# Deformable convolutions: the clamp of the distances on POOL instead of DVE, and the middle one of three sampled parts read by DVE instead of ACT

## The reference

```
_block: h      = relu(conv3x3(x))
        offset = conv3x3(h)                       # 9 taps x (y, x) per pixel
        x      = relu(deform_conv(h, offset, w))  # bilinear samples of h, then a sum over taps and channels
layers 1 to 3 take x + (input of the layer before)
final:  cat(x, input) (64 channels) -> offset = conv3x3 -> deform_conv, added to the input
```

## Time and profile before

| | |
|---|---|
| median of 3 runs | 4874.02 us (4866.67 to 4875.91) |
| profiled execution, its own time | 4847.23 us |
| its span | 4845.4 us |
| mean granted TensorE clock | 0.913 |
| chunks of the layer steps | 8 x 32, starts of the sums some 8.5 us apart |
| chunks of the final steps | 2 x 32, some 26 us apart |

### The profile page before, as it was taken

How to read it: one execution, slowest core, us unless ns; L and a number is a source line. 1 busy time by engine, 2 the same in 40 slices (tenths; PEclk the granted TensorE clock), 3 DMA queues, 4 the chain that set the end, 5 groups by cost and what they waited for, 6 DMA issues and landing times.

```text
span 4845.4 us, 204328 instructions
## 1 busy us (share of the span) xinstructions
PE 4248.1 (88%) x73184; PEld 3301.6 (68%) x73184; DVE 2918.2 (60%) x5838; ACT 2784.3 (57%) x6651; POOL 1143.4 (24%) x655
## 2 busy tenths in 40 slices
PE   4997997898798798798799799698989887999988
PEld 3775675676576576576576577577777776777777
DVE  4884784785685686686586587354444535554544
ACT  2893884785685586586587488244343433344433
POOL 0441341341341242242243143011111101111110
PEclk8998998899899899899899799799899998888998
DMA  3442442442442442443343343744444436444442
GB/s 123 121 125 74 121 125 76 117 125 69 125 125 72 121 124 78 119 125 86 110 125 92 102 125 103 185 111 109 101 109 109 100 92 157 112 103 107 111 111 77
DMA packets 253669, 533.42 MB, mean 110 GB/s; under 512 B 61488, under 2 KB 161328, under 8 KB 235824
## 3 DMA queue, kind: packets, MB, share of 16 engines
q1 hardware_dynamic: 253072, 524.86, 41.1%
HBM read 468.16 MB, written 56.45 MB: 108 GB/s over the span
## 4 chain that ended last, share of the span: by engine, by line
PE 79%; issue 8%; SPq 6%; ACT 2%; DMA 2%; DVE 2%; POOL 1%; POOLq 0%; ACTq 0%; PEld 0%; DVEq 0%; PEldq 0%
PE P L531 30%; PE PS L545 25%; PE PS L557 17%; PE P L502 6%; SPq L383 2%; SPq L375 2%; ACT H L790 1%; DMA HB<-off_store 1%; PE PS L502 1%; DMA off_store<-FOFF 1%; ACT YC L727 1%; DVE FOFF L974 1%; DVE ST L977 0%; DVE ST L978 0%; PE P L517 0%
## 5 line engine op out<-in xcount | busy, mean ns | idle before, releaser
L857 DVE TENSOR_TENSOR A<-P,YC 121x384 f32<-121x384 f32 (+1 forms) x4608 | 2313.5, 551 | 1327.0 <-ACT YC L727 1041.9
L531 PE MATMUL P<-HL,SEL 32*121 32x384 f16 (+1 forms) x21504 | 1738.6, 309 | 336.3 <-issue 236.3
L727 ACT ACTIVATE YC<-P 121x384 f32<-121x384 f32 (+1 forms) x4608 | 1739.8, 439 | 100.4 <-PE P L531 88.5
L531 PEld LDWEIGHTS P<-HL,SEL 32*121 32x121 f16 (+1 forms) x21504 | 1195.1, 119 | 734.1 <-issue 420.5
L545 PE MATMUL PS<-A,VT 121*32 121x144 f32 (+1 forms) x32768 | 1339.3, 304 | 71.5 <-issue 47.4
L545 PEld LDWEIGHTS PS<-A,VT 121*32 121x32 f32 (+1 forms) x32768 | 963.4, 115 | 381.9 <-issue 202.0
L1038 POOL CAST HL<-DIST 128x1152 f16<-128x1152 f32 x320 | 365.8, 1143 | 3437.3 <-DVE DIST L862 3203.8
L704 ACT ACTIVATE SMP<-PS 128x432 f32<-128x432 f32 (+1 forms) x1152 | 567.5, 493 | 722.7 <-PE PS L545 721.8
L557 PE MATMUL PS<-SMP,CW 128*128 128x128 f32 x6912 | 856.6, 280 | 5.2 <-ACT SMP L704 5.2
L557 PEld LDWEIGHTS PS<-SMP,CW 128*128 128x128 f32 x6912 | 795.7, 192 | 87.3 <-issue 76.9
L1040 POOL TENSOR_TENSOR HL<-DIST,HL 128x1152 f16<-128x1152 f32 x320 | 769.3, 2404 | 135.2 <-issue 76.0
(11 more groups left out here) (56 smaller groups left out, 581.2 us busy)
## 6 DMA issues: line engine op xcount, KB each, us to landing
HB<-off_store SPq DMA_DIRECT2D x2560, 72.0 KB, 2.4
VT<-ht_store SPq DMA_DIRECT2D x256, 512.0 KB
VT<-ht_store SPq DMA_DIRECT2D x768, 132.0 KB
VT<-ht_store SPq DMA_DIRECT2D x256, 88.0 KB
ht_store<-A SPq DMA_DIRECT2D x80, 256.0 KB, 3.4
off_store<-FOFF SPq DMA_DIRECT2D x160, 128.0 KB, 2.5
A<-x_dram SPq DMA_DIRECT2D x2, 2048.0 KB, 10.2
H<-x_dram SPq DMA_DIRECT2D x2, 2048.0 KB, 15.6
```

The lines of the kernel that those rows point to most:

```text
L531: mm = nc.tensor.matmul(dst, SEL[q, table, 0:sh.npos], hats, start=part == 0, stop=part == 1)
L727: nc.scalar.activation(YC[0:sh.npos, g % X_SLOTS, 0:sh.size], P[0:sh.npos, g % Y_SLOTS, 0:sh.size], ACT.Copy).then_inc(y_ready, 1)
L857: return nc.vector.tensor_tensor(dst, x, y, ALU.mult)
```

## The change

The clamp leaves DVE's queue (behind product 1, and ahead of offset item 4) and stands on POOL ahead of the cast: POOL waits for the abs, clamps, waits for its own clamp, casts, and subtracts as before. In kind 0 with one source (the layer steps), the part with index 1 is no longer read by ACT behind its copy of g = 7 but by DVE behind product 7, by a `tensor_copy` from PSUM. The final steps keep all reads on ACT; their clamp moves too. In the tail of a step, DVE's read stands between the two last residuals.

```diff
--- before.py
+++ after.py
@@ -88,6 +88,8 @@
         self.after = {2: [4, 9], 3: [4, 7, 10], 6: [2, 4, 6, 8, 10, 11]}[count]
 
         self.sum_after = 1
+
+        self.dve_parts = [1] if count == 3 and kind == 0 else []
 
         self.lag = 3 - self.batches
         self.ps_uses = self.batches * count + 1
@@ -732,7 +734,7 @@
                                 continue
                             else:
                                 prev = (c - 1, sh.batches - 1)
-                            if g in sh.after:
+                            if g in sh.after and sh.after.index(g) not in sh.dve_parts:
                                 read_part(*prev, sh.after.index(g))
                             if b == sh.batches - 1 and g == sh.sum_after and before >= sh.lag:
                                 read_sum(c - sh.lag, (half + sh.lag) % 2)
@@ -741,7 +743,8 @@
                     if sh.lag == 2:
                         read_sum(CHUNKS - 2, 0)
                     for k in range(nparts):
-                        read_part(CHUNKS - 1, sh.batches - 1, k)
+                        if k not in sh.dve_parts:
+                            read_part(CHUNKS - 1, sh.batches - 1, k)
                     read_sum(CHUNKS - 1, 1)
 
                 chunk_loop(act, body, tail)
@@ -856,11 +859,6 @@
                     y = y.broadcast_to(list(x.shape))
                 return nc.vector.tensor_tensor(dst, x, y, ALU.mult)
 
-            def clamp(c):
-
-                dve.wait_ge(abs_done, c + 1)
-                nc.vector.tensor_scalar(DIST[:, :], DIST[:, :], SCALE, SCALE, ALU.min, ALU.subtract).then_inc(clamp_done, 1)
-
             def body_of(sh, layer, group, final):
                 nparts = len(sh.parts)
 
@@ -870,6 +868,12 @@
                     x = P[0:sh.npos, Y_SLOTS + g % X_SLOTS, 0:sh.tiles * sh.size].rearrange("p (n a) -> p n a", n=sh.tiles)
                     a = A[0:sh.npos, half if sh.kind == 0 else b, :].rearrange("p (n a) -> p n a", n=sh.tiles)
                     return product(sh, a[:, :, at:at + sh.size], x, YC[0:sh.npos, g % X_SLOTS:g % X_SLOTS + 1, 0:sh.size])
+
+                def read_part(c, k):
+                    w, s = sh.parts[k][0]
+                    count = len(sh.parts[k])
+                    dve.wait_ge(ps_full, c * sh.ps_uses + k + 3)
+                    nc.vector.tensor_copy(smp_px(0, sh, w, s, count), PS[:, 0:TAPS * BPX * count]).then_inc(ps_free, 1)
 
                 def add_residual(c, band, half):
 
@@ -889,8 +893,8 @@
                             dve.wait_ge(y_ready, n + 1 + Y_SLOTS)
                             dve.wait_ge(x_full, n + 2)
                             one_product(g, b, half).then_inc(product_done, 1)
-                            if b == 0 and g == 1 and not last:
-                                clamp(c + 1)
+                            if before > 0 and b == 0 and g in sh.after and sh.after.index(g) in sh.dve_parts:
+                                read_part(c - 1, sh.after.index(g))
                             if before >= sh.lag and b == sh.batches - 1 and g == sh.sum_after + 2:
                                 if sh.lag == 2:
                                     add_residual(c - 2, band - 1, half)
@@ -900,6 +904,8 @@
                 def tail():
                     if sh.lag == 2:
                         add_residual(CHUNKS - 2, BANDS - 1, 0)
+                    for k in sh.dve_parts:
+                        read_part(CHUNKS - 1, k)
                     add_residual(CHUNKS - 1, BANDS - 1, 1)
 
                 def input_back(c, band, half, before, last):
@@ -965,8 +971,6 @@
                 for n in range(ITEMS):
 
                     unit, image = divmod(n, IMG)
-                    if n == IMG:
-                        clamp(0)
                     dve.wait_ge(off_full, unit + 1)
                     if n >= OFF_SLOTS:
 
@@ -1034,6 +1038,8 @@
 
             def hats(c, half):
 
+                wait_alone(pool, abs_done, c + 1)
+                nc.gpsimd.tensor_scalar(DIST[:, :], DIST[:, :], SCALE, SCALE, ALU.min, ALU.subtract).then_inc(clamp_done, 1)
                 wait_alone(pool, clamp_done, c + 1)
                 nc.gpsimd.tensor_copy(HL[:, 0, half, :], DIST[:, :]).then_inc(hat_step, 1)
                 wait_alone(pool, hat_step, c + 1)
```

## The result

The changed kernel takes 5446.75 us (median of 4 runs, 5431.56 to 5461.90) against 4870.35 (4864.88 to 4875.91): ratio 1.1183 [1.1149, 1.1218]. Slower was the likeliest side of the forecast, but 4902 is far off and the time lies 297 us above the top of the range. The profiled execution took 5445.4 us (span 5443.6; 4847.2 and 4845.4 before), so 598 us have to be found.

A forecast was written before the change was run, and what follows sets the result against it. The prediction took a resynchronised chunk of 8.5 us as the pitch, to be set by the third sample waiting for DVE's read. 29 + 1 - 2 = +28 us on 4874 gave 4902; forecast's own range 4885 to 4940, whole range 4860 to 5150.

The forecast's parts named there:

- The clock as no issue: Steady loop of the kernel before: granted clock 1.00, the 2.4 GHz level, so no clock loss was priced.
- Clamp off DVE: DVE's queue: removing the 0.75 us clamp saves 0 per chunk, and 2 us in all at step starts.
- Clamp onto POOL: POOL, ahead of the cast: POOL has time, order matters; with a 1.25 us clamp the residual just gets in.
- D: Duration of POOL's clamp: taken as 1.25 us, between ends of 0.75 and 2.41.
- A + 5.33 + D: Time the hats are ready on POOL, A being the start of the chunk's abs.
- Rival 1: POOL's subtraction gets ahead of DVE's residual: 5148 us with every second chunk hit, 5331 with every chunk; chance 0.22.
- knife edge: Residual against POOL's subtraction: at 1.25 us of clamp the subtraction starts 4.31 or 4.45 after the sums' start, residual 4.31.
- S + 4.31: Predicted start of DVE's residual in a chunk, S being the start of the sum matmuls.
- Rival 2: POOL's clamp is long, so the residual waits for the cast: 5009 us at 2.0 us, 5104 at 2.41; chance 0.13.
- Middle read onto DVE: DVE behind product 7: a 0.60 us read delays the third sample; 0.125 per chunk, 29 us over 232 chunks.
- Rival 3: DVE reads early enough for the third sample (start by S + 6.1), spreads lose their waits: 4823 us; chance 0.13.

The follow-up runs named there:

- late_only: Kernel before, with the layer steps' residual moved in DVE's queue behind the chunk's last product: 4868.95 us, ratio 0.9998.
- quick_late: Kernel before with a 1.15 us POOL multiply-and-add replacing DVE's clamp (values not clamped), reads on ACT, residual behind the last product: 4864.50 us, ratio 1.0002.
- quick2: Kernel before with two POOL multiplications (2.5 us together) replacing DVE's clamp, values not clamped; reads on ACT, residual in its old place: 5006.56 us, ratio 1.0327.
- after_late: Changed kernel with the layer steps' residual moved behind product 11, the chunk's last: 5405.95 us, ratio 1.1110.
- quick_both: Changed kernel with a 1.15 us multiply-and-add in place of POOL's clamp (values not clamped), middle read on DVE: 5472.60 us, ratio 1.1247.
- quick_clamp: Kernel before with a 1.15 us POOL multiply-and-add replacing DVE's clamp (values not clamped), all reads on ACT, residual in its old place: 5303.87 us, ratio 1.0894.
- clamp_only: Changed kernel with the middle read back on ACT, so only the clamp moves to POOL: 5284.60 us, ratio 1.0867.
- read_only: Kernel before with only the middle part's read moved to DVE, clamp still on DVE: 4981.51 us, ratio 1.0245.
- read_late: Kernel before with the middle read on DVE and the layer steps' residual behind product 11, clamp still on DVE: 4904.51 us, ratio 1.0077.

## Why the prediction was wrong

**The clock as no issue.** It was read from the kernel before and held for it. The forecast and every rival priced a late step by its own microseconds at the full clock. After the change PE stops in every steady chunk (0.66 us in the mean), and the sums' group is busy 1036.1 us instead of 856.6: 180 of the 598 us, 1.94 in a chunk whose sums are slow throughout and less in the others. The chunks that have such sums are longer by more than that, 12.2 instead of 9.71, together 264 us; what else than the clock makes them long is not separated. No rival had this term.

**Clamp off DVE: nothing gained.** This held. late_only against quick_late, 0.9998 and 1.0002, differ in little but where the clamp's time lies, although quick_late has no clamp on DVE at all.

**Clamp onto POOL: this step failed.** The term D, for which the forecast had ends of 0.75 and 2.41 and said "I take 1.25", measured 4.09. The form was not in the trace, and the bound from above was taken from another kind of instruction. The formula behind it was right: A + 5.33 + D gives A + 9.42, measured A + 9.44, and its condition, hats in time "for D up to 2.4", agrees with what was run: at D = 2.5 the granted clock stayed 1.00 and 8 sums of 256 were slow (quick2), at 4.09 PE waited for the hats. With the right D the step would have read: abs to abs 9.70, 232 x (9.70 - 8.5) = 278 us, and to that the half clock, which only a run gives.

**Rival 1.** In the changed kernel it is a small part of the cause (after_late gives back some 40 us). Its mechanism exists as described: at D = 1.15 residuals of 2.55 us end 0.15 behind the subtraction, and quick_late takes all of the price away. The forecast was wrong on where the knife edge lies; by its own numbers, residual and subtraction both at S + 4.31, it was a tie in one chunk of two. It counted on one chunk of two; 216 of 256 were hit: the chunk shown has sums at the full clock and both instructions start at S + 4.25, and behind sums at the half clock the residual comes later still, while the subtraction runs. Its price for the whole change with every chunk hit was 5331 (with D = 0.75 its formula gives delays of 1.73 and 1.87, so 418 us and not 429); quick_both, the whole change with most chunks hit (199 of 256), took 5473. That quick_clamp's 5304 is nearer is chance, as it has no DVE read.

**Rival 2.** Right in kind, as quick2 shows at the length it was priced for. Beyond that length its price does not go on growing: the residual, blocked in 106 of 320 cases in clamp_only, costs nothing measurable there; PE waits for the late hats in any case.

**Middle read onto DVE: +28, measured 120 alone.** The read took the forecast 0.60 and the third sample waits for it. The forecast gave the residual 0.34, for a kernel in which POOL's cast is over before it; in read_only the clamp stays on DVE, the residual meets the cast, and that is some 80 of the 120. Where the residual is out of the way, the read costs 37 us without the POOL clamp (read_late, 1.0077) and some 58 with the short one (1.0002 to 1.0121), so the term was near. Two errors in it partly cancel: in read_late the third sample came at S + 7.03, not 7.19, and the next sums 1.63 behind it, not 1.44. On top of the 4.09 us clamp the same read costs some 155 us (ratios 1.0867 and 1.1183); that each wait it adds falls on a PE that already stops is a reading, not a test.

**Rival 3** falls: in the changed kernel the read starts at S + 7.26 in the median, not by S + 6.1. With the residual out of the way it started at S + 6.39, and the kernel was still no faster.

**The residual and POOL.** The Trainium skill, "SBUF — State Buffer", section "Who interferes with whom", has the whole instruction shut out the other engine. For the cast and the subtraction the traces agree (ends 0.15 behind them). For the 4.09 us clamp they do not: in the chunk shown the residual ended at 1039.32 and the clamp at 1039.51, and in 100 cases of clamp_only it ended some 0.2 before the clamp. What the clamp does in its last 0.2 us no run shows, and the profile's spans on POOL are rough. The Trainium skill, "GPSIMD Engine Reference", section 3.1, gives bodies of at most two operations 1.03 cycles per element: the forecast's estimate from it, 0.99 us plus overhead, holds for multiply-and-add (1.15) and not for minimum-and-subtract (4.09), and the measurement decides.

Open: of the steady chunks' 527 us, the distance of 9.71 accounts for 262, and the longer chunks with half-clock sums for the other 264. No run held the clock while the hats were late, so the two shares are counted in the trace and not separated by a run.

## What to carry to other kernels

An instruction form that the trace does not show has no bound from its neighbours: ask for its duration with one probe before moving it to another engine, and look at what the other engines do while the probe runs. Where two engines shut each other out, a shorter instruction can cost more than a longer one (5304 us at 1.15, 5007 at 2.5), as it sets which of the others' instructions it meets; here the small residual, which two tensors feed, cost nothing once it stood where POOL did not read. And when PE is close to never waiting, look for the clock that a delay may cost too: stops of 0.34 to 1.43 us went with sums of 3.90 to 4.21 us for 2.27 in the chunks shown, though one stop of 0.45 in every chunk of read_only did not.

## What was not expected of the hardware

POOL's tensor_scalar on 128x1152 f32 costs 1.15 us for multiply-and-add, 3.1 to 3.2 for one operation, and 4.1 for min with subtract or add, for add with min and for max with multiply. No run says why. Multiply with min or subtract took 6.0 to 6.1, and min-and-subtract 4.05 on 576 elements, each while DVE wrote 128x4096 elements from A to X; less that overlap the estimates are 4.0 and 2.0. Without such a neighbour min-and-subtract took 1.18 on 288. The overlap costs DVE as well: its instruction took 2.42 us alone, and 4.48 and 5.81 behind POOL's.
